# A GNN kernel that fetches node rows by one-hot products: plain fp32 in place of two float32r parts

## The reference

```python
# layer 0
h = x @ W_lin + b_lin
h = tanh(mean_aggregate(h, src, dst) @ W1_agg + h @ W1_root + b1)
x = layernorm(x + tanh(mean_aggregate(h, src, dst) @ W2_agg + h @ W2_root + b2))
# layer 1
h = x @ Wn.T + bn
w = ssp(ssp(edge_feats @ We1.T + be1) @ We2.T + be2)       # ssp: softplus - log 2
agg = segment_sum(h[src] * w, dst)
x = layernorm(x + ssp(agg @ Wc.T + bc) @ Wp.T + bp)
```

## Time and profile before

| | |
|---|---|
| median of 3 runs | 8767.93 us (8767.54 to 8774.95) |
| profiled execution: span | 8760.1 us (no other time is given of it) |
| mean granted TensorE clock | 0.951 |
| TensorE matmul, weight load | 7637.1 us (87%), 6905.6 us (79%) |
| DVE, ScalarE, POOL | 5505.1 (63%), 5860.1 (67%), 6259.5 us (71%) |

### The profile page before, as it was taken

The page is one execution under the profiler, slowest core; times in us unless marked ns, Lnnn a source line. Parts: engine busy times, 40 slices in busy tenths (PEclk is TensorE's granted clock), DMA queues, the critical chain, the costliest instruction groups (busy, mean ns, idle before and its releaser), DMA issues. The chain is left out here.

```text
span 8760.1 us, 165117 instructions
## 1 busy us (share of the span) xinstructions
PE 7637.1 (87%) x51516; PEld 6905.6 (79%) x51517; DVE 5505.1 (63%) x7447; ACT 5860.1 (67%) x10176; POOL 6259.5 (71%) x6471
## 2 busy tenths in 40 slices
PE   7999999999989999999999777777777777888887
PEld 6999999888889999998888666666666666776775
DVE  5655656666645555556666666666666666777777
ACT  5777777666657777776666566666666666666665
POOL 5777777766557777777664477777777777777776
PEclk9999999999989999999999798988988889999999
DMA  2111112111111111111111222222222222222222
GB/s 75 35 34 35 35 34 35 31 30 28 25 40 34 35 34 35 34 34 31 31 30 23 75 56 59 55 57 57 55 58 56 55 59 55 55 59 56 55 56 59
DMA packets 341135, 392.62 MB, mean 45 GB/s; under 512 B 165119, under 2 KB 240563, under 8 KB 340564
## 3 DMA queue, kind: packets, MB, share of 16 engines
q0 software_dynamic: 204000, 151.96, 12.1%
q1 hardware_dynamic: 136750, 239.87, 8.1%
q10 hardware_dynamic: 322, 0.03, 0.0%
HBM read 375.47 MB, written 15.92 MB: 45 GB/s over the span
## 5 line engine op out<-in xcount | busy, mean ns | idle before, releaser
L699 PE MATMUL banks<-split_sb,e_low_hot 128*128 128x400 f32 x22000 | 4092.6, 346 | 45.6 <-DVE split_sb L752 45.6
L699 PEld LDWEIGHTS banks<-split_sb,e_low_hot 128*128 128x128 f32 x22000 | 4015.6, 189 | 74.1 <-DVE split_sb L752 46.1
L922 POOL DMA_INDIRECT big<-hn_table,src_i x2875 | 2857.0, 994 | 883.7 <-issue 870.7
L645 POOL DMA_INDIRECT big<-p_table,src_i x1750 | 1655.8, 946 | 695.2 <-issue 528.7
L758 DVE TENSOR_REDUCE picked<-banks 128x48 f32<-128x1200 f32 x1000 | 1300.1, 1300 | 1352.1 <-PE banks L699 1351.1
L670 ACT ACTIVATE e_low_hot<-e_key_off 128x1536 fp32r<-128x1536 f16 x1000 | 1381.1, 1381 | 1130.6 <-PE banks L699 1112.7
L645 POOL DMA_INDIRECT big<-h_table,src_i x1750 | 1674.9, 957 | 612.5 <-issue 529.6
L666 ACT ACTIVATE e_key_off<-e_key_in,node_off 128x384 f16<-128x384 f16 (+1 forms) x4000 | 2028.4, 577 | 125.5 <-DMA e_key_in<-sel_dram 41.4
L957 PE MATMUL banks<-hn_split,e_low_hot 128*128 128x448 f32 x7000 | 1500.1, 370 | 75.5 <-issue 70.1
L957 PEld LDWEIGHTS banks<-hn_split,e_low_hot 128*128 128x128 f32 x7000 | 1298.0, 188 | 217.1 <-issue 96.6
L781 DVE TENSOR_TENSOR hot<-e_dst_pair,banks 128x1536 bf16<-128x1536 bf16 (+1 forms) x934 | 931.1, 997 | 69.9 <-issue 0.6
(11 more groups left out here) (216 smaller groups left out, 4491.7 us busy)
## 6 DMA issues: line engine op xcount, KB each, us to landing
e_wide<-in_edge_t SPq DMA_DIRECT2D x125, 832.0 KB
e_key_in<-sel_dram SPq DMA_DIRECT2D x250, 343.8 KB
big<-hn_table,src_i POOLq DMA_INDIRECT x2875
big<-p_table,src_i POOLq DMA_INDIRECT x1750
big<-h_table,src_i POOLq DMA_INDIRECT x1750
e_key_in<-gate_dram SPq DMA_DIRECT2D x125, 64.0 KB
src_i<-in_src SPq DMA_DIRECT2D x375, 12.5 KB, 1.7
e_key_in<-sel_dram SPq DMA_DIRECT2D x250, 8.2 KB
```

The source lines that it names most:

```text
L645: pool.indirect_dma_start(buf[u][:, j, 0:ROW0], None, table, bass.IndirectOffsetOnAxis(ap=src_i[u][:, j:j + 1], axis=0),).then_inc(gathere ...
L699: last = pe.matmul(o, low_hot[gr][:, h, e], split_sb[:, part, h * HI1:(h + 1) * HI1, :], start=(h == 0 and part == 0), stop=(h == HI2 - 1 ...
L922: pool.indirect_dma_start(buf[u][:, j, 0:F], None, table, bass.IndirectOffsetOnAxis(ap=src_i[u][:, j:j + 1], axis=0),).then_inc(gathered[u ...
```

## The change

The picks become one plain fp32 product per one-hot with the whole table. The float32r type, the split tables and the code that makes them go. In e1 and e2 the table is copied from where its DMA lands into `table_sb`; in e3 stage c writes `hn_all` with the bias add, and the DMA into `hn_table` reads it from there.

```diff
-        split_sb = mid.enter_context(nc.sbuf_tensor("split_sb", [P, 2, HI1 * HI2, H], F32R))
+        table_sb = mid.enter_context(nc.sbuf_tensor("table_sb", [P, HI1 * HI2, H], F32))
...
-                for part in range(2):
-                    dve.tensor_scalar(split_sb[:, part].rearrange("p (h a) f -> p h a f", h=HI2),
-                                      away[:, :, 0:HI1].unsqueeze(3).to_broadcast([P, HI2, HI1, H]),
-                                      1.0 - part, None, ALU.mult)
+                dve.tensor_copy(table_sb[:, :, :].rearrange("p (h a) f -> p h a f", h=HI2),
+                                away[:, :, 0:HI1].unsqueeze(3).to_broadcast([P, HI2, HI1, H]))
...
-            low_hot = [tiles.enter_context(nc.sbuf_tensor(f"{tag}_low_hot{gr}", [P, HI2, SIZE[gr] * P], F32R))
+            low_hot = [tiles.enter_context(nc.sbuf_tensor(f"{tag}_low_hot{gr}", [P, HI2, SIZE[gr] * P], F32))
...
                             for h in range(HI2):
-                                for part in range(2):
-                                    last = pe.matmul(o, low_hot[gr][:, h, e],
-                                                     split_sb[:, part, h * HI1:(h + 1) * HI1, :],
-                                                     start=(h == 0 and part == 0), stop=(h == HI2 - 1 and part == 1))
+                                last = pe.matmul(o, low_hot[gr][:, h, e], table_sb[:, h * HI1:(h + 1) * HI1, :],
+                                                 start=(h == 0), stop=(h == HI2 - 1))
...
-                    pe.wait_ge(split_made, 4)
+                    pe.wait_ge(table_made, 2)
...
-                    def split_table():
-                        tops, rests = [split_sb[0:PR, part].rearrange("p (h a) f -> p a h f", h=HI2) for part in range(2)]
-                        dve.wait_ge(split_in, 32)
-                        scratch = h1_deg[0:PR, :, :].rearrange("p n c -> p (n c)")
+                    def place_table():
+                        rows_of = table_sb[0:PR].rearrange("p (h a) f -> p a h f", h=HI2)
+                        dve.wait_ge(table_in, 32)
                         for h in range(2):
-                            at = slice(FULL_CUT[h], FULL_CUT[h + 1])
-                            top = scratch[:, HI2 * H * FULL_CUT[h]:HI2 * H * FULL_CUT[h + 1]].rearrange(
-                                "p (a h f) -> p a h f", h=HI2, f=H)
-                            dve.tensor_single_scalar(top.bitcast(I32), full_in[h].bitcast(I32), TOP12, ALU.bitwise_and)
-                            dve.drain()
-                            dve.tensor_copy(tops[:, at], top).then_inc(split_made, 1)
-                            dve.tensor_tensor(rests[:, at], full_in[h], top, ALU.subtract).then_inc(split_made, 1)
+                            dve.tensor_copy(rows_of[:, FULL_CUT[h]:FULL_CUT[h + 1]], full_in[h]).then_inc(table_made, 1)
...
                         for h in range(GLOW):
-                            for part in range(2):
-                                for c in range(2):
-                                    last = pe.matmul(bank[c][:, 0:GHALF * F], low_hot[s][:, h, :],
-                                                     hn_split[:, part, h * GHIGH + c * GHALF:h * GHIGH + (c + 1) * GHALF, :],
-                                                     start=(h == 0 and part == 0), stop=(h == GLOW - 1 and part == 1))
+                            for c in range(2):
+                                last = pe.matmul(bank[c][:, 0:GHALF * F], low_hot[s][:, h, :],
+                                                 hn_all[:, h * GHIGH + c * GHALF:h * GHIGH + (c + 1) * GHALF, :],
+                                                 start=(h == 0), stop=(h == GLOW - 1))
...
-                    if g >= 2:
-                        dve.wait_ge(f_store[g % 2], 16 * (g // 2))
-                    dve.tensor_tensor(hn_o[g % 2][:, 0:b - a, :], by_node(bank[5 + g % 2], b - a),
+                    dve.tensor_tensor(hn_all[:, a:b, :], by_node(bank[5 + g % 2], b - a),
                                       bn_all[:, :].unsqueeze(1).to_broadcast([P, b - a, F]), ALU.add).then_inc(f_out, 1)
-                    if g >= 2:
-                        dve.wait_ge(f_hi, g - 1)
-                    t = top_i[g % 2][:, 0:b - a, :]
-                    dve.drain()
-                    dve.tensor_single_scalar(t, hn_o[g % 2][:, 0:b - a, :].bitcast(I32), TOP12,
-                                             ALU.bitwise_and).then_inc(f_top, 1)
-                    dve.drain()
-                    dve.tensor_tensor(hn_split[:, 1, a:b, :], hn_o[g % 2][:, 0:b - a, :], t.bitcast(F32), ALU.subtract)
...
-                    if g >= 3:
-                        a, b = group(g - 3)
-                        act.wait_ge(f_top, g - 2)
-                        act.copy(hn_split[:, 0, a:b, :], top_i[(g - 3) % 2][:, 0:b - a, :].bitcast(F32)).then_inc(f_hi, 1)
...
-                    sp.dma_start(hn_v[:, a:b, :], hn_o[g % 2][:, 0:b - a, :]).then_inc(f_store[g % 2], 16)
+                    sp.dma_start(hn_v[:, a:b, :], hn_all[:, a:b, :]).then_inc(f_store[g % 2], 16)
```

More of the change, by code:

```diff
@@ L13 @@
 F32 = mybir.dt.float32
-F32R = mybir.dt.float32r
 I32 = mybir.dt.int32
@@ L75 @@
 PICK = HI1 * H
-TOP12 = -4096
 BIG = 2.0 ** 126
@@ L587, in pick_phase @@
             pick_psum = sem(f"{tag}_pick_psum")
-            split_in = sem(f"{tag}_split_in")
-            split_made = sem(f"{tag}_split_made")
+            table_in = sem(f"{tag}_table_in")
+            table_made = sem(f"{tag}_table_made")
             pick_taken = sem(f"{tag}_pick_taken")
@@ L629, in _ @@
                                      [:, HI2 * FULL_CUT[h]:HI2 * FULL_CUT[h + 1], :].rearrange("p c f -> p (c f)")
-                                     ).then_inc(split_in, 16)
+                                     ).then_inc(table_in, 16)
                     keys(1, 1)
@@ L815, in _ @@
                     dve.sem_inc(pick_taken, 2)
-                    split_table()
+                    place_table()
                     for gr in range(3):
@@ L843, in gate_phase @@
             key_in = [tiles.enter_context(nc.sbuf_tensor(f"{tag}_key_in{u}", [P, GSEL * P], F16)) for u in range(2)]
-            low_hot = [tiles.enter_context(nc.sbuf_tensor(f"{tag}_low_hot{s}", [P, GLOW, P], F32R)) for s in range(GSEL)]
+            low_hot = [tiles.enter_context(nc.sbuf_tensor(f"{tag}_low_hot{s}", [P, GLOW, P], F32)) for s in range(GSEL)]
             high = tiles.enter_context(nc.sbuf_tensor(f"{tag}_high", [P, GSEL, GHIGH], F32))
@@ L1293, in gnn_kernel @@
         hn_held = ExitStack()
-        hn_split = hn_held.enter_context(nc.sbuf_tensor("hn_split", [P, 2, NQ, F], F32R))
-        f_top = sem("f_top")
-        f_hi = sem("f_hi")
+        hn_all = hn_held.enter_context(nc.sbuf_tensor("hn_all", [P, NQ, F], F32))
         f_xb = sem("f_xb")
@@ L1307, in gnn_kernel @@
         x1, st_sum, st_mean, var, rstd, sq = norm_tiles("c")
-        tanh_w = [tiles.enter_context(nc.sbuf_tensor(f"tanh{b}", [P, GQ, F], F32)) for b in range(3)]
-        tanh_t = [t[:, 0:CQ, :] for t in tanh_w]
-        top_i = [t[:, :, :].bitcast(I32) for t in tanh_w[0:2]]
+        tanh_t = [tiles.enter_context(nc.sbuf_tensor(f"tanh{b}", [P, CQ, F], F32)) for b in range(3)]
         x1T = [tiles.enter_context(nc.sbuf_tensor(f"x1T{b}", [P, GQ * F], F32)) for b in range(2)]
-        hn_o = [tiles.enter_context(nc.sbuf_tensor(f"hn_o{b}", [P, GQ, F], F32)) for b in range(2)]
         def pack(t, k):
@@ L1438, in _ @@
                 act.activation(rstd[:, :], rstd[:, :], ACT.Exp, scale=-0.5).then_inc(f_rstd, 1)
-                for g in range(NGQ + 3):
-                    if g < NGQ:
-                        a, b = group(g)
-                        act.wait_ge(f_xT_psum, g + 1)
-                        if g >= 2:
-                            act.wait_ge(f_hn_psum, g - 1)
-                        act.copy(x1T[g % 2][:, 0:(b - a) * F], bank[3 + g % 2][:, 0:(b - a) * F]).then_inc(f_xT, 1)
-                    if g >= 3:
-                        a, b = group(g - 3)
-                        act.wait_ge(f_top, g - 2)
-                        act.copy(hn_split[:, 0, a:b, :], top_i[(g - 3) % 2][:, 0:b - a, :].bitcast(F32)).then_inc(f_hi, 1)
+                for g in range(NGQ):
+                    a, b = group(g)
+                    act.wait_ge(f_xT_psum, g + 1)
+                    if g >= 2:
+                        act.wait_ge(f_hn_psum, g - 1)
+                    act.copy(x1T[g % 2][:, 0:(b - a) * F], bank[3 + g % 2][:, 0:(b - a) * F]).then_inc(f_xT, 1)
             @block.gpsimd
```

## The result

The kernel after takes 12,357.7 us (median of 4 runs, 12,357.6 to 12,358.8), the kernel before 8768.4 us (4 runs, 8767.5 to 8775.0). The ratio is 1.409, with a 95% interval of 1.407 to 1.411. The profiled execution has a span of 12,355.7 us at a mean granted clock of 0.989; its own time is 12,357.6 us.

A forecast was written before the change was run, and what follows sets the result against it. TensorE was taken to bound e1 and e2, POOL's gathers e3. From the 8760.1 us span, + 3366 - 10 + 281 - 18 - 7 gave 12,372; with 7.8 us carried over, 12,380 us (+41%), range 12,250 to 12,560.

The forecast's parts named there:

- e1 and e2: The two pick phases, bound by TensorE: 22,000 passes longer by 336 - 183 ns, +3366 us, all on the path.
- e3: Gate phase: bound moves from POOL's gathers (29.8 us a block) to TensorE (30.6 us); 3746 to 4027 us, +281 us.
- The price of a pass: Plain fp32 picks: two cycles a column plus 2.5 ns, so 336 ns at 400 columns and 376 ns at 448.
- adding up: TensorE's idle time between block visits in the two pick phases: -10 us for both, between 0 and -30.
- a second visit: Gate phase: 46 blocks have one, about 4.1 us each, no longer covered by POOL; 45 x 4.1 = 185 us counted.
- The middle stage and the tables: Dropped mask, subtraction and copies: -18 us in the middle stage (-12 to -22), -7 us for the tables.
- (a): Picks: float32r's surcharge stays on plain passes, 350 and 395 ns, total 12,810 us; chance 6%.
- (b): Gate phase hides its growth: blocks stay at the gathers' 29.8 us, total 12,110 us; chance 4%.
- (c): Clock stays at half under plain picks: passes of 669 and 749 ns, total 22.6 ms; chance 2%.
- (d): A plain pass costs picks what a float32r pass does; only copies and masks go, 8733 us; chance 1%.

The follow-up runs named there:

- e3_plain: The kernel before with plain fp32 picks in the gate phase and the lighter middle stage alone: 9035.1 us, ratio 1.031.
- e3_pick0: The kernel before with only the first pick of each gate-phase block plain, reading the table's upper part alone: 8817.9 us, ratio 1.0062.

## Why the prediction was right

*The price of a pass.* This was the term that decided, and it came out to the nanosecond: 336 and 376 ns. It was read from L940, another shape with other operands, by two ways (half clock and full clock) that gave the same two cycles a column. The counts were as forecast. e1 and e2 together moved by 3332 us, where 22,000 x 153 = 3366 less 10 was forecast. That these are only 24 us apart is in part luck, for two terms missed in opposite directions. The smaller one is adding up, in the kernel before:

```profile
L717 PE MATMUL banks<-hot,big 128*64 128x128 bf16 x8550 | 376.0, 226 | 209.1 <-DVE acc L805 114.0
```

Busy and idle time are 585 us there and 529 us at L711: adding up takes 56 us less, where 10 was put down and 30 was the bound. Its wait for DVE's one-hots falls from 77.3 to 47.8 us, as the longer pick 0 hides more of them, and its wait for `acc` rises from 114.0 to 136.5. The rest is its busy time, which the forecast left as it was; why it is less is not traced. A block's first visit now takes 0.84 us with no wait (161.92 to 162.76). So the picks grew by 3332 + 56 = 3388 us, 154 ns a pass with the gaps between them.

*e3.* The bound changed hands as forecast: no wait at L927, the clock at 0.99, POOL waiting for buffers. The block of 30.73 us shown above was forecast at 30.6, the one with two visits (34.64) at 34.7. The sum of +281 measured +286, although a second visit was put down at 4.1 us, where the earlier trace rows give 4.19 and the two blocks now differ by 3.91. e3_plain shows that this term stands by itself. The same reasoning failed once, in e3_pick0 (54 us for an expected 25 at most), because the slack of the 46 blocks with a second visit is smaller than the 5 us seen in a block with one; in the prediction the second visits had a term of their own, and there it held.

*The middle stage and the tables.* -15.7 for -18, -4.2 and -3.5 for -4 and -3. In the kernel after, two groups of eight in the middle stage, and the table's copies:

```profile
8241.53 0.66 PE L1334 MATMUL banks<-ident,c_x 128*128 128x128 f32 x4
...
8243.21 0.66 PE L1334 MATMUL banks<-ident,c_x 128*128 128x128 f32 x4
```
```profile
90.25 1.49 DVE L739 COPY table_sb<-hot 125x832 f32<-125x832 f32 x2 [14.46 <-DMA hot<-p_full]
```

A group takes 1.68 us (3.40 in the earlier trace rows); 1.8 was forecast. The first pick begins 1.6 us after the landing (91.80), 4.8 in the earlier trace rows.

*The rivals.* (a) is out: 336 ns and not 350, and the bf16 passes show whose surcharge it is. (b) is out: blocks of e3 are at TensorE's 30.7 us. (c) is out: 0.99 in all three windows, so the 0.50 of 4830 to 4890 us belongs to that stretch and not to plain fp32 at large. (d) is out: two cycles a column with one-hot weights as well. The Trainium skill (FP8 and Floating Point Precision, TensorE Precision Notes) says that true fp32 takes four passes through the array; two records of two cycles a column are four cycles a column for the product, and the rows bear it out, while two float32r products take two and 2 x 16 ns.

## What to carry over

Before swapping several reduced-precision matmuls for one full-precision one, count the instructions and the cycles a column on both sides in a trace: a plain fp32 product of 400 columns cost 672 ns, two float32r products 366 and two bf16 ones 338. If such a row is missing for the shape, another shape's at the same clock will do for plain fp32, whose price went by columns from 208 to 448; float32r's did not (111 to 114 ns at 208 columns, 183 at 400). What a longer pass costs is read from the stage: all of it where TensorE is the bound (e1, e2: 3332 of 3366 us), a quarter where gathers hide the rest (e3: 286 of 1181 us), and a block's slack must be taken from its tightest kind.

## What the runs showed of the hardware that was not expected

- float32r passes cost 16 ns above one cycle a column (183 ns at 400 columns), bf16 passes 2.5 ns (169), with the same one-hots in the same loop. Where the 16 ns come from is open.
- In two of the five series the kernel before took 8764 and 8768 us at a mean granted clock of 0.95, in three 12,525 to 12,688 us at 0.80 to 0.81. In the traces from the slower ones, all of changed kernels, TensorE is idle in issue at the picks and the first layer, and at adding up, which no edit touched (L974: 960.5 us; but 18.8 us with three bf16 parts), and hardly at the second layer (L947: 0.7 us). What holds its instructions back is not settled; that the time goes more by their number (102 to 116 ns for a pass and its load) than by their length is what the runs show.
